# Chunk 0 of the last attention finished ahead of the other targets, and Pool's additions given to VectorE

## The reference

```
x = x + gat(layernorm(x), adj)          # graph attention, 4 heads, a softmax for each head
x = x + moe8(layernorm(x))              # top 2 of 8 experts, 128 -> 512 -> 128
# second graph attention: four heads' scores averaged, one softmax
z = s1[:, None, :] + s2[None, :, :];  e = where(z > 0, z, 0.2 * z).mean(-1)
attn = softmax(where(adj > 0, e, -9e15), axis=1);  x = x + attn @ (x @ W.T)
# second mixture, a route for every 32 rows, HID = 256
h = relu(layernorm(x) @ Wi.T + bi)
for l in 0, 1:
    h = relu(h @ Ws[l].T + bs[l] + h @ Wr[l, route].T + br[l, route] + h)
x = x + h @ Wo.T + bo
```

## Time and profile before

| what | value |
|---|---|
| median of 3 runs (lowest to highest) | 630.83 us (628.54 to 633.81) |
| profiled execution: own time / span | 632.04 / 630.3 us |
| mean granted clock of TensorE | 0.941 |
| busy: PE, PEld, DVE, ACT, POOL | 86%, 68%, 82%, 59%, 28% |

### The profile page before, as it was taken

The page is one execution under the profiler, slowest core; times in us unless marked ns, Lnnn a source line. Parts: engine busy times, 40 slices in busy tenths (PEclk is TensorE's granted clock), DMA queues, the critical chain, the costliest instruction groups (busy, mean ns, idle before and its releaser), DMA issues.

```text
span 630.3 us, 13281 instructions
## 1 busy us (share of the span) xinstructions
PE 542.1 (86%) x5082; PEld 429.6 (68%) x5082; DVE 516.3 (82%) x907; ACT 372.2 (59%) x756; POOL 178.9 (28%) x186
## 2 busy tenths in 40 slices
PE   1979777999999999799998897999996855899985
PEld 1768674978866877667686565578886645567753
DVE  6799999997797756899849728999999899999630
ACT  1699795768885787586755745542331401566473
POOL 3311000165311201984522010021315000364941
PEclk9989896989998999899998899899999688799999
DMA  6485930022245346999598215020201844476750
GB/s 141 88 166 109 260 83 1 18 86 85 89 133 197 107 133 219 221 212 237 110 209 97 68 23 180 2 68 0 68 1 42 298 144 141 121 224 190 211 178 18
DMA packets 48857, 78.36 MB, mean 124 GB/s; under 512 B 5406, under 2 KB 24870, under 8 KB 48794
## 3 DMA queue, kind: packets, MB, share of 16 engines
q1 hardware_dynamic: 30714, 52.02, 26.2%
q0 software_dynamic: 15488, 22.02, 20.5%
q10 hardware_dynamic: 2592, 3.48, 1.9%
HBM read 80.61 MB, written 22.06 MB: 163 GB/s over the span
## 4 chain that ended last, share of the span: by engine, by line
PE 46%; DVE 31%; ACT 10%; issue 5%; POOL 3%; DMA 2%; SPq 1%; ACTq 0%; POOLq 0%; DVEq 0%
DVE arena L1641 17%; PE bank L698 13%; PE bank L710 10%; PE bank L627 10%; PE bank L867 4%; ACT arena L1143 3%; DVE arena L1464 3%; ACT ysb L1095 2%; POOL x L550 2%; DVE arena L1468 1%; PE bank L824 1%; DMA routed_sums<-in_wsT 1%; PE bank L603 1%; PE bank L576 1%; PE bank L808 1%
## 5 line engine op out<-in xcount | busy, mean ns | idle before, releaser
L483 POOL TENSOR_TENSOR x<-x,ysb 128x512 f32<-128x512 f32 x36 | 75.9, 2107 | 245.5 <-ACT ysb L1095 233.5
L1143 ACT ACTIVATE arena<-heads,nd 128x512 bf16<-128x512 f32 x176 | 111.8, 720 | 21.4 <-PE bank L627 21.0
L698 PE MATMUL bank<-hTc,arena 128*128 128x512 f32 x192 | 95.9, 656 | 5.6 <-ACT reg_c L1084 5.6
L1641 DVE SCALAR_TENSOR_TENSOR arena<-reg_b,nd,arena 128x1536 f32<-128x1536 f32 x48 | 92.0, 1977 | 0.0
L710 PEld LDWEIGHTS bank<-arena,reg_c 128*128 128x128 f32 x768 | 87.6, 192 | 4.8 <-issue 4.7
L710 PE MATMUL bank<-arena,reg_c 128*128 128x128 f32 x768 | 88.5, 276 | 0.0
L1084 ACT ACTIVATE reg_c<-bank,b 128x512 f32<-128x512 f32 x96 | 65.3, 687 | 25.8 <-PE bank L698 25.7
L627 PEld LDWEIGHTS bank<-reg_b,arena 128*128 128x128 bf16 x1536 | 73.4, 99 | 7.0 <-DVE arena L1497 4.0
L627 PE MATMUL bank<-reg_b,arena 128*128 128x99 bf16 x1536 | 74.6, 211 | 3.8 <-DVE arena L1497 3.8
L1095 ACT ACTIVATE ysb<-bank,comb 128x128 f32<-128x128 f32 x128 | 36.5, 367 | 65.5 <-PE bank L913 39.9
L698 PEld LDWEIGHTS bank<-hTc,arena 128*128 128x128 f32 x192 | 39.2, 211 | 52.7 <-issue 44.3
(11 more groups left out here) (195 smaller groups left out, 844.7 us busy)
## 6 DMA issues: line engine op xcount, KB each, us to landing
maskT<-routed_sums SPq DMA_DIRECT2D x48, 256.0 KB, 3.2
reg_c<-in_adj POOLq DMA_DIRECT2D x16, 512.0 KB, 7.1
arena<-in_w1T SPq DMA_DIRECT2D x16, 512.0 KB, 3.9
arena<-in_w2T SPq DMA_DIRECT2D x16, 512.0 KB, 4.8
routed_sums<-in_wsT SPq DMA_DIRECT2D x32, 256.0 KB, 5.5
routed_sums<-in_wrT POOLq DMA_DIRECT2D x32, 256.0 KB, 12.7
arena<-routed_sums SPq DMA_DIRECT2D x32, 256.0 KB, 3.0
routed_sums<-ident POOLq DMA_DIRECT2D x4, 1024.0 KB, 12.7
```

The source lines that it names most:

```text
L483: nc.gpsimd.tensor_tensor(xi, xi, ysb[:, e % 3, :].rearrange("p (t d) -> p t d", d=P), ALU.add).then_inc(s_acc, 1)
L698: mm(bank[b][:, :], w1[:, s, e % 2, c * P:(c + 1) * P], hTc[:, :], start=True, stop=True).then_inc(full[b], 1)
L1143: last = af(ind[:, q, b, j, :], sbc[:, h, :], ACT.Relu, bias=nd[:, q * QT + j, h:h + 1], scale=BIG)
L1641: last = v.scalar_tensor_tensor(p, row, nd[:, t, h:h + 1], p if h else maskT[:, t, columns], ALU.max, ALU.mult)
```

## The change

Five things are done together.

1. `scale` signals after each tile and `ln_transpose` waits tile by tile; in the inverse root one scaling is folded into another instruction.
2. Source tiles 12 to 15 are multiplied for chunk 0's 512 columns first (`s_c0`), then for head 0 of the other 1024 columns; chunk 0 is merged and normalised from its own sums (`s_c0sums`), and the other heads follow. TensorE runs the first pair, whose tiles use banks 4 to 7, ahead of `attend_part` for the other targets and of the attentions 0 and 1. Source tiles 2 and 3 of chunk 3's targets go behind the norms of chunks 1 and 2.
3. Pool no longer adds anything to x. `bo` is a third part of the biases that TensorE brings in with the one-hot matmul, in the outputs too. ScalarE still copies outputs of chunks 0 to 2 to `ysb`, in two slots; VectorE adds a chunk in one instruction. The last four tiles are added by VectorE out of PSUM. SyncE stores, chunk 3 in three parts.
4. VectorE waits for the selections 3, 4 and 5 behind head 0 of source tiles 4 to 7, 8 to 11 and 12 to 15.
5. Twelve of the `kept` tiles are loaded before the first mixture has ended; other loads of SyncE and ScalarE's wait for `kept` move with the new order. The attention lists move on by about one pair, and ScalarE copies chunk 3's sums ahead of the outputs of tiles 10 and 11, not of 8 and 9.

```
 # w_second
+            if t < 2:
+                return (arena[:, 8848:9360], arena[:, 9360:9872], hT[:, WW:N], ysb[:, 2, :],
+                        *(rows1[:, h, 0:CW] for h in range(H)))[m].rearrange("p (k n) -> p k n", k=KC)
...
+        def tile_banks(t):
+
+            return ((4, 5), (6, 7))[t] if t < 2 else (2 + t % 2 * 2, 3 + t % 2 * 2)
...
 # SyncE
+            sp.wait_ge(s_skip, 16 * L * KC)
+            for e in range(T - CT):
+                load_kept(e)
             sp.wait_ge(s_acc, FFN_Y)
...
+            sp.wait_ge(ev["rows"], 3 * H)
+            load_second(0)
+            sp.wait_ge(s_c0, CT)
+            load_second(1)
+            for e in range(T - CT, E1):
+                load_kept(e)
             load_second(2)
             load_second(3)
             sp.wait_ge(full[3], BANK3)
-            load_second(0)
-            load_second(1)
...
+            for c in range(C - 1):
+                sp.wait_ge(s_acc, FFN_Y + c + 1)
+                store(c * CT, CT)
+            for t0, n in ((T - CT, 2), (T - 2, 1), (T - 1, 1)):
+                sp.wait_ge(ev["y"], FFN_Y + t0 + n)
+                store(t0, n)
...
 # GpSimd
-                nc.gpsimd.tensor_tensor(xi, xi, bo.unsqueeze(1).to_broadcast([P, CT, P]),
-                                        ALU.add).then_inc(s_xb, 1)
...
-                    nc.gpsimd.tensor_tensor(xi, xi, ysb[:, 0, i * P:(i + 1) * P], ALU.add).then_inc(s_acc, 1)
...
+            for t in range(2, T, 2):
+                select(t)
+                if t in (CT + 2, 2 * CT + 2):
+                    pool.wait_ge(*layer_done(t - 3, L))
+                    one_hot((t - 2) // CT + 1)
...
 # TensorE
             def ln_transpose(b=6, src=xn):
-                pe.wait_ge(s_xn, k.event("xn"))
                 use(b, "hTc")
                 for i in range(CT):
+                    pe.wait_ge(s_xn, k.event("xn"))
...
+            def attend_part(targets, t, ready):
+
+                pe.wait_ge(s_v1, C)
+                pe.wait_ge(ready, t + 1 if ready is s_wide else t - (T - CT) + 1)
+                for i in targets:
+                    b, o = i // 3, i % 3 * (P + 1)
+                    last = mm(bank[b][:, o:o + P + 1], wide[:, t % 4, i * P:(i + 1) * P], v1[:, t, :], start=False,
+                              stop=(t == T - 1), skip_group_check=True)
...
-            for g in range(5, T // 2):
-                attend_wide(g)
-            attend1(0)
-            attend1(1)
+            attend_wide(5)
+            for t in range(T - CT, T):
+                attend_part(range(CT), t, s_c0)
...
             ln_transpose(6, odiv)
             expert_pair(0, 0, ((), (), ()))
-            expert_pair(0, 2, ((2,), (3,), ()), xn)
-            expert_pair(1, 0, ((), (4,), ()))
-            expert_pair(1, 2, ((5, 6, 7), (8,), ()), odiv)
-            expert_pair(2, 0, ((9, 10), (11, 12, 13), (14, 15)))
+            pe.wait_ge(s_c0sums, 1)
+            for t in range(T - CT, T):
+                attend_part(range(CT, WT), t, s_wide)
+            attend1(0)
+            attend1(1)
+            expert_pair(0, 2, ((), (), ()), xn, 1)
+            expert_pair(1, 0, ((2,), (3,), ()))
+            expert_pair(1, 2, ((4,), (5, 6), (7,)), odiv)
+            expert_pair(2, 0, ((8,), (9, 10, 11), (12, 13, 14, 15)))
...
 # ScalarE
-                        if i == 0 and l == 1 and c == C - 2:
-                            sums(3 * (P + 1), P + 1)
...
+                    if (c, i) == (C - 2, 2):
+                        sums(3 * (P + 1), P + 1)
+                    for t in pair:
+                        output(t)
+                    if (c, i) == (0, 0):
+                        act.wait_ge(s_kept, 16 * E1)
+                        select(3, range(GT))
+                        other_sums()
...
 # VectorE
                 for h in range(H):
+                    if selected and h == 1:
+
+                        dve.wait_ge(s_even, selected)
...
+            def add_chunk(c):
+
+                dve.wait_ge(ev["y"], FFN_Y + (c + 1) * CT)
...
+            for g in (6, 7):
+                dve.wait_ge(s_exp, 3 + g // 2)
+                dve.wait_ge(s_widef, g - 1)
+                for h in range(H):
+                    products(h, (2 * g, 2 * g + 1), wide[:, :, 0:CW], rows1[:, h, 0:CW], slice(0, CW), s_c0)
...
+            other_targets(0)
+            dve.wait_ge(ev["att"], (2 * C + 1) * H + 1)
+            dve.wait_ge(s_c0sums, 1)
+            divisors(CT, att)
+            then(merge1(0, CT, 0, att))
+            norm(0, 2 * C + 4, odiv)
+            for h in range(1, H):
+                other_targets(h)
...
+            last_tiles(2, 2)
+            last_tiles(4, QT, 3)
+            last_tiles(8, QT, 4)
+            add_chunk(0)
+            last_tiles(12, QT, 5)
+            add_chunk(1)
...
+            add_chunk(2)
+            for t in range(T - CT, T):
+                dve.wait_ge(*layer_done(t, L))
+                v.tensor_tensor(x[:, t, :], x[:, t, :], bank[3 + t % 2 * 2][:, 0:P], ALU.add).then_inc(ev["y"], 1)
```

More of the change, by code:

```diff
@@ L408, in _, with store @@
             sp.wait_ge(full[3], BANK3)
-            load_second(0)
-            load_second(1)
-            for t in range(4, T):
-                sp.wait_ge(full[3 + t % 2 * 2], (BANK5 if t % 2 else BANK3) + (t - 4) // 2 * (L + 1) + L)
+            load_second(4)
+            load_second(5)
+            for t in range(6, T):
+                sp.wait_ge(*layer_done(t - 4, L - 1))
                 load_second(t)
+            outv = out.rearrange("(t p) d -> p t d", p=P)
+            def store(t0, n):
+                sp.dma_start(outv[:, t0:t0 + n, :], x[:, t0:t0 + n, :]).then_inc(s_out, 16)
+            for c in range(C - 1):
[4 more added lines that the diff above has]
+                store(t0, n)
+            sp.wait_ge(s_out, 16 * (C + 2))
         @block.gpsimd
@@ L518, in _ @@
             pool.wait_ge(s_pool, 6)
-            outv = out.rearrange("(t p) d -> p t d", p=P)
             def one_hot(c):
@@ L870, in layer, with turn @@
                 last.then_inc(full[b], 1)
-            def turn(i):
-                b = 2 + i % 2 * 2
-                ready(b + 1)
+            def turn(t):
+                i, (b, b1) = t % CT, tile_banks(t)
+                ready(b1)
                 use(b, "htt")
@@ L962, in expert_pair @@
                 for t in pair:
-                    hidden(t % CT)
+                    hidden(t)
                 for l in range(L):
@@ L968, in expert_pair @@
                         layer(t, l)
-                    if l == 0 and then is not None:
+                    if l == at and then is not None:
                         ln_transpose(6, then)
@@ L1295, in _, with other_sums, hidden @@
             scale_values(3)
-            sums(*[3 * (P + 1)] * (WT // 3), to=reg_b)
-            def hidden(i):
-                b = 2 + i % 2 * 2
+            act.wait_ge(s_attf, C * H)
+            got(0)
+            af(att[:, 0:3 * (P + 1)], bank[0][:, 0:3 * (P + 1)], ACT.Copy).then_inc(ev["att"], 1)
+            got(1)
+            af(att[:, 3 * (P + 1):CT * (P + 1)], bank[1][:, 0:P + 1], ACT.Copy).then_inc(s_c0sums, 1)
+            k.event("sums")
+            def other_sums():
+                o = CW
+                for b in range(1, WT // 3):
+                    got(b)
+                    w = slice(P + 1 if b == 1 else 0, 3 * (P + 1))
+                    af(reg_b[:, o:o + w.stop - w.start], bank[b][:, w], ACT.Copy).then_inc(ev["att"], 1)
+                    o += w.stop - w.start
+            def hidden(t):
+                i, b = t % CT, tile_banks(t)[0]
                 got(b)
@@ L1690, in _, with other_targets @@
             wide_pair(5, range(H - 1, H))
-            for g in range(6, T // 2):
-                wide_pair(g)
+            for g in (6, 7):
[3 more added lines that the diff above has]
+                    products(h, (2 * g, 2 * g + 1), wide[:, :, 0:CW], rows1[:, h, 0:CW], slice(0, CW), s_c0)
+            def other_targets(h):
+                products(h, range(T - CT, T), wide[:, :, CW:WW], rows1[:, h, CW:WW], slice(CW, WW), s_wide)
+            other_targets(0)
[6 more added lines that the diff above has]
+                other_targets(h)
             dve.wait_ge(ev["rows"], 3 * H)
@@ L1697, in _ @@
             dve.wait_ge(ev["att"], (2 * C + 1) * H + WT // 3)
-            divisors(WT, reg_b)
-            then(merge1(0, CT, 0, reg_b))
-            norm(0, 2 * C + 4, odiv)
-            last_tiles(2, 2)
-            merge1(CT, 2 * CT, CT, reg_b).then_inc(s_attf, 1)
+            rest = reg_b[:, CW:]
+            divisors(2 * CT, rest)
+            merge1(CT, 2 * CT, 0, rest).then_inc(s_attf, 1)
             dve.wait_ge(s_attf, C * H + 1)
```

178 lines of the change are left out of this document (87 added, 91 removed).

## The result

The changed kernel takes 640.01 us (median of 4 runs, 639.17 to 642.06), the kernel before 631.66 on the same chip: a ratio of 1.0141, with a 95% interval of 1.0089 to 1.0193. It is slower by 8.4 us. The profiled execution took 639.19, its span is 637.2. The forecast was 637.5.

The account below looks back on a forecast made before the run. Two chains were taken to arrive together at 604.5: TensorE's pairs with Pool's stall, and VectorE's products plus last normalisation. Terms 2.5 + 6.3 + 2.0 - 2.8 - 1.2 = 6.8 gave 637.5 us; range 628 to 643.5.

Parts of the forecast that it names:

- late sums: Before chunk 3: sums copied one pair later leave merge and norm uncovered, 17.5 us between hidden layers instead of 11.16, +6.3.
- three signs of being wrong: Products end before 589, gap before chunk 3's transposes under 3 us, or VectorE standing several us at the selection waits.
- VectorE 5.6 later at the first pair's end: Chunk 0's source tiles 12 to 15: 3.8 us stall, 2.4 for cutting products, selection traffic, less 0.85.
- Products' end +3.7: VectorE's last products end at 594.4 against 590.7, with less Pool work beside them and selection waits put at nothing.
- rival 2: Pool starves: selections wait until VectorE stops at each of three waits, 3.3 us each; 643 us, chance 0.13.
- The pair's hidden layer +2.5: Last pair before chunk 3: TensorE waits for VectorE's products, then attentions and outputs; hidden layer at 597.8 against 595.26.
- Low clock in chunk 3 +2.0: Chunk 3's first pair, behind an idle TensorE, takes 11.3 us instead of 9.27; between 0 and 2.5.
- Tail -2.8: Kernel's end: fewer output copies, and a short addition with SyncE's issue and landing, save 2.8 us, between 2 and 4.
- Tile-wise waits -1.2: First chunk and first mixture's end: transposes waiting for their tile, not the chunk, save 1.2 us, between 0 and 1.6.
- Rival 1: VectorE's products are not the limit; the pair starts with TensorE at 593, 4.8 us less: 632.7 us, chance 0.22.
- Rival 3: First pair and Pool's stall come off with little lost, some 7 us gained: 623.5 us, chance 0.15.
- rival 4: First pair's overlap fails through late second-layer weights or ScalarE's queue; under 3 us late costs nothing; no separate chance given.

Follow-up runs that it names:

- stores-on-Pool run: Changed kernel with its six output stores and their waits issued from Pool's queue instead of SyncE's: 641.36 us, ratio 1.0178.
- test without waits: Changed kernel without VectorE's three waits for Pool's selections: 647.57 us, ratio 1.0266.
- sums early: Changed kernel with ScalarE's copies of chunk 3's sums moved back ahead of the outputs of tiles 8 and 9: 631.96 us, ratio 0.9997.
- attentions later: Changed kernel with its last four attentions moved to the first half of the pair of tiles 10 and 11, sums right behind: 627.98 us, ratio 0.9954.
- kept busy: Changed kernel with unread matmuls, five ahead of the last attentions and six ahead of chunk 3's transposes: 636.9 us, ratio 1.0118.
- first two experiments: Changed kernel with chunk 3's sums copied one pair earlier, 631.96 us; kernel before with only those copies moved later, 639.07 us.
- the last one: Kernel with later attentions, selections by DMA, VectorE's selection waits removed, plus one VectorE wait for chunk 2's one-hot cast: 627.98 us, ratio 0.9927.
- DMAs: Kernel with later attentions, Pool's four selection copies made DMAs of Pool's queue, VectorE's three waits removed: 636.36 us, ratio 1.0069.

## Why the prediction was right

By number the forecast was 637.5 for 640.01, inside its range; its mechanism, the late sums on an idle TensorE, is what the experiments show. One of its own three signs of being wrong came all the same: VectorE stood 4.4 us at the selection waits. The other two did not (the products did not end before 589, and the gap before chunk 3's transposes is 6.94). Behind the norm point the forecast's terms sum to 8.0 (without the 1.2 of the front), measured were 10.5, or some 8.5 with the last matmul where the stores-on-Pool run has it. Term by term, from the profile of after:

- **VectorE 5.6 later at the first pair's end: right.** The stall was 3.96 for 3.8. VectorE had the narrow source tiles done and went on at 537.53, 52.2 behind the norm point; the forecast's 541.8 is 52.8 behind 488.99. So it was 5.0 later.
- **Products' end +3.7: 6.0.** This is the term that failed. The step was "The waits themselves I put at nothing", with the reason that the pair that lets Pool select starts 3 us ahead of the wait. From there to the end VectorE took 55.5 instead of 52.6, with 4.37 of it at two waits, and 1.4 less in the work itself. From two stretches of before I had taken that selections run beside products; here they began 2.1 and 4.9 us ahead of the wait and were held at their first copy. That is the mechanism of rival 2, at 2.2 us for each of two waits instead of 3.3 for each of three. The test without waits shows it: 23.32 us for one selection. The size is partly chance: in four other profiles with the same order up to there (sums early, attentions later, stores on Pool, kept busy) the third selection got its turns, took 3.7 us instead of 7.49, and the products ended 106.2 to 106.5 behind the norm point, 4.5 to 4.8 later than before, where after has 107.7.
- **The pair's hidden layer +2.5: 6.8** (4.5 in the stores-on-Pool run). 2.3 is the term above. The rest, some 2, is the clock: the forecast had allowed some of it for four attentions, they took 6.22 against 3.84 kept busy.
- **Late sums +6.3: 17.48 - 11.16 = 6.3.** The parts hold too: 9.85 us from the hidden layer to the reciprocal, where the forecast had 9.4 + 0.65, and 7.63 from there to chunk 3's hidden layer, where it had 6.5 + 0.9. That the sum fits to the tenth is chance. The first two experiments show the cause in both directions; the intervals that they give differ from 6.3 (7.3 less, 8.6 more), and in the median the move is worth 8, with the clock.
- **Low clock in chunk 3 +2.0: 10.52 - 8.54 = 2.0** (from 606.42 to 614.96 in the timeline of before), and 1.9 less when TensorE is kept busy.
- **Tail -2.8: -4.5** from the last pair's hidden layer to the end (10.82 for 15.34). Behind the last matmul it is 2.3 us, where before had 6.4 and the forecast 4. I had looked only at issue and landing. SyncE's stores of 64 KB land in 1.5 us, where I had taken the 2.0 of a load of 128 KB; and the 2.03 us of Pool's closing step, which I had not seen, went off the path.
- **Tile-wise waits -1.2: nothing that can be seen.** Where the time goes was not traced.

The sum came out 2.5 us short behind the norm point, and the median too; the tail, 1.7 better than forecast, hid part of what the hidden layer lost (4.3). That errors partly cancelled is luck. The largest term, the late sums, was right in place and size, and it alone decides the sign. Rival 1 (VectorE not the limit) is false for this kernel, true for the last one. Rival 3's gains are real but hidden: with the late sums undone the time is that of before, and only with the attentions in another pair does some of it come out. The overlap came about, against rival 4.

The Trainium skill (SBUF — State Buffer, Who interferes with whom) says that a VectorE instruction with two inputs in SBUF contends with a Pool instruction that reads SBUF, and that whoever issues first has the ports for that instruction, the other blocked. The kind of pair agrees with these traces. So does the length once a copy has got in: from 552.22 in the kernel before copies and products went turn by turn, one copy and one product in about 1.0 us. It does not for a first copy: one copy was held 21.66 us, over some 30 products in a row, not over one. The page also says, as an inference, that making descriptors needs only the write side, which such products leave free; the trace agrees, with Pool's issues, in the last run, at 0.54 us each beside products of 743 ns each, where the view by groups of the kernel before has 831 to 877 for the same products beside copies.

Open: what lets a first copy in. In the kernel before selections mostly got their turns (28 copies at 784 ns, at the price of slower products), in the changed one they mostly waited, and the third selection of the changed kernel did either, from one profile to the next. The order in which the two engines issue is a candidate that wasn't tried. Open too is what moves the norm point by 10 us between executions.

## What to carry to other kernels

When a step moves work of one engine forward, look at what stands in the queues of the others on the way back: here a copy moved by one pair cost all that the overlap of a whole pair had brought. Price an idle stretch of TensorE of some 6 us at its length and some 2 us of slower work behind it (1.6 to 2.4 here), and fill it with a part of the next step. A wait put on a busy engine so that another gets its turn can be cheaper than none; take the neighbour's work off that engine altogether before you take out the wait, and look which small operation then takes the starved place. Let the last store of a program be issued by an engine that can end at once: here SyncE and not Pool, 2.9 us in the profile.

## What the runs showed of the hardware

- A Pool operation that reads SBUF could be held through a long run of VectorE's two-input products: one copy 13.39 us (after) and 21.66 (no waits), a cast 15.96 (DMAs), an addition 8.86 (before). Each ended within 1.2 us of the run's end, whether VectorE then idled or only did an addition between. Once one was in, the copies behind it took turns with the products, one of each in about 1.0 us.
- Behind 5.83 and 6.94 us without work TensorE's granted clock was 0.74 and 0.75 in the two windows shown; 32 matmuls took 6.22 us for 3.84. Matmuls without a use in the gap brought back 2.4 and 1.9 us against after, 1.6 and 1.6 against the stores-on-Pool run.
- Output stores of 64 KB landed in 1.5 us when SyncE issued them and in 2.0 by Pool (median of two each), the one of 128 KB in 1.8 and 2.7.
- Pool's closing step took 2.03 us (before) and 2.19 (stores on Pool) and stood behind its last store; SyncE's took 7 ns (after).
